# Causal self-attention inside a decoder layer: score units handled four at a time, eight slots of exponentials

## The reference

```python
q = (xq @ wq.T + bq).reshape(Bq, Tq, H, hd).transpose(0, 2, 1, 3)
...
scores = jnp.einsum('bhqd,bhkd->bhqk', q, k) / jnp.sqrt(jnp.asarray(hd, xq.dtype))
scores = scores + bias[None]            # relative position, and -inf above the diagonal
attn = jax.nn.softmax(scores, axis=-1)
out = jnp.einsum('bhqk,bhkd->bhqd', attn, v)
```

## Time and profile before

| | |
|---|---|
| median of 3 runs | 2869.88 us (2867.36 to 2872.76) |
| the profiled execution | 2871.87 us |
| its span in the trace | 2870.0 us |
| TensorE matmul busy | 2732.3 us (95% of the span) |
| VectorE busy | 1600.8 us (56%) |
| ScalarE busy | 1238.6 us (43%) |
| mean granted TensorE clock | 0.979 of full speed |

### The profile page before, as it was taken

How to read it: one execution, slowest core, us unless ns; L and a number is a source line. 1 busy time by engine, 2 the same in 40 slices (tenths; PEclk the granted TensorE clock), 3 DMA queues, 4 the chain that set the end, 5 groups by cost and what they waited for, 6 DMA issues and landing times. The chain is left out here.

```text
span 2870.0 us, 40053 instructions
## 1 busy us (share of the span) xinstructions
PE 2732.3 (95%) x12704; PEld 1797.9 (63%) x12704; DVE 1600.8 (56%) x3852; ACT 1238.6 (43%) x2624; POOL 410.2 (14%) x494
## 2 busy tenths in 40 slices
PE   7999969999999999999999889899989999999998
PEld 6788844444444444444444467667767778777877
DVE  5554356777777777777777188467632222122211
ACT  2322113555555555555555344498822222332222
POOL 4000021000000000000000422188555000000000
PEclk9999978999999999999999999899999999999999
DMA  7656563222222222222221587645331000000000
GB/s 223 225 181 195 184 150 78 66 67 67 68 68 68 68 69 68 68 68 67 67 67 25 120 229 223 213 150 170 125 121 44 15 30 30 30 0 30 30 15 15
DMA packets 137822, 272.53 MB, mean 95 GB/s; under 512 B 24773, under 2 KB 54725, under 8 KB 132362
## 3 DMA queue, kind: packets, MB, share of 16 engines
q1 hardware_dynamic: 132394, 254.57, 31.1%
q0 software_dynamic: 5216, 15.33, 1.9%
HBM read 175.44 MB, written 99.98 MB: 96 GB/s over the span
## 5 line engine op out<-in xcount | busy, mean ns | idle before, releaser
L1140 ACT ACTIVATE sa_pr<-sa_st 128x512 f32<-128x512 f32 (+3 forms) x1280 | 610.6, 532 | 562.2 <-DVE sa_st L1203 316.3
L1108 PE MATMUL sa_ov<-sa_pr,sa_v 128*33 128x512 f32 (+3 forms) x2560 | 537.7, 541 | 0.0
L1189 DVE TENSOR_REDUCE sa_part<-sa_mp 128x1 f32<-128x512 f32 (+3 forms) x768 | 411.8, 583 | 116.2 <-PE sa_mp L1089 115.0
L1099 PE MATMUL sa_st<-sa_q,sa_k 97*128 97x512 f32 (+3 forms) x1280 | 442.1, 414 | 16.6 <-ACT sa_pr L1140 13.1
L1099 PEld LDWEIGHTS sa_st<-sa_q,sa_k 97*128 97x128 f32 x1280 | 217.2, 190 | 318.8 <-ACT sa_pr L1140 211.3
L1089 PE MATMUL sa_mp<-sa_k,sa_q 96*128 96x512 f32 (+3 forms) x1280 | 373.5, 386 | 26.0 <-DVE sa_mp L1167 20.2
L1841 PE MATMUL ff_o<-ff_w,ca_q 128*128 128x512 f32 x1536 | 379.7, 396 | 3.4 <-DVE ca_q L1894 3.4
L1186 DVE CUSTOM_DVE_ANT_0 sa_mp<-sa_mp,sa_ub 128x512 f32<-128x512 f32 (+3 forms) x512 | 317.7, 663 | 79.3 <-PE sa_mp L1089 68.4
L1894 DVE TENSOR_TENSOR ca_q<-ca_v,ca_q 128x512 fp32r<-128x512 f32 x128 | 93.3, 729 | 474.6 <-ACT ca_q L1877 474.6
L130 PE MATMUL ff_f<-ff_ln_hi,ff_w 128*128 128x512 f32 x1024 | 340.9, 394 | 3.5 <-DVE ff_ln_lo L255 3.5
L1841 PEld LDWEIGHTS ff_o<-ff_w,ca_q 128*128 128x128 f32 x1536 | 287.1, 188 | 74.4 <-DVE ca_q L1894 3.6
(11 more groups left out here) (198 smaller groups left out, 3302.1 us busy)
## 6 DMA issues: line engine op xcount, KB each, us to landing
sa_q<-scratch_q SPq DMA_DIRECT2D x96, 256.0 KB, 8.3
sa_k<-scratch_k SPq DMA_DIRECT2D x96, 256.0 KB, 8.9
scratch_q<-qkv_qst SPq DMA_DIRECT2D x32, 512.0 KB, 7.2
scratch_k<-qkv_qst SPq DMA_DIRECT2D x32, 512.0 KB, 5.7
scratch_q<-sao_qst SPq DMA_DIRECT2D x32, 512.0 KB, 3.8
ca_q<-scratch_q SPq DMA_DIRECT2D x32, 512.0 KB, 4.2
scratch_v<-qkv_vst SPq DMA_DIRECT2D x8, 1056.0 KB, 5.2
sa_v<-scratch_v SPq DMA_DIRECT2D x16, 528.0 KB, 12.9
```

Source lines behind the costliest of these rows:

```text
L1099: pe.matmul(st[bank(u, h)][:, 0:w], ks[n.par][:, h, kb * P:(kb + 1) * P], qs[n.par][:, h, g * GW + c0:(g + 1) * GW], start=True, stop=True ...
L1108: last = pe.matmul(ov[64 * h:64 * h + VW, c0:GW], vs[n.par][:, kb, h, :], pr[:, u % 4, h, 0:GW - c0], start=(u in opens), stop=(u in ends))
L1140: act.activation(pr[:, u % 4, h, 0:w], st[bank(u, h)][:, 0:w], ACT.Exp, scale=SCALE).then_inc(s["exp"], 1)
L1189: dve.tensor_reduce(to, tile, AX_X, ALU.max).then_inc(s["red"], 1)
```

## The change

Units are handled in blocks of BATCH = 4 in place of 2, on all three engines: scores(u+4) with the max steps of u, scores(u+5) with those of u+1, and so on to scores(u+7), then the values of u to u+3. Eight slots of exponentials take the place of four, so exponent(u) waits for values(u-8). Three of the eight lie in `early[5]`, five in a tile of their own. Four units open the first slot in place of two. The number of score banks (3), the tables and the steps after each unit stay as they are.

```diff
+    BATCH = 4
...
-        for v in (u + 2, u + 3):
+        for v in range(u + BATCH, u + 2 * BATCH):
...
-        pr = k.sb(f"{name}_pr", [P, 4, 2, GW])
+        own = k.sb(f"{name}_pr", [P, 2 * BATCH - 3, 2, GW])
+        pr = [early[5][:, 2 * GW * i:2 * GW * (i + 1)].rearrange("p (h t) -> p h t", h=2) for i in range(3)]
+        pr += [own[:, i] for i in range(2 * BATCH - 3)]
...
-                                     pr[:, u % 4, h, 0:GW - c0], start=(u in opens), stop=(u in ends))
+                                     pr[u % len(pr)][:, h, 0:GW - c0], start=(u in opens), stop=(u in ends))
...
-            scores(Step(0, 0, UNROLL), 0)
-            scores(Step(0, 0, UNROLL), 1)
+            for u in range(BATCH):
+                scores(Step(0, 0, UNROLL), u)
 
             def slot(n, left):
-                for u in range(0, NU, 2):
+                for u in range(0, NU, BATCH):
                     ahead = list(after(n, u, left))
-                    for i in range(2):
+                    for i in range(BATCH):
                         if ahead:
                             scores(*ahead[i])
                         for m, a in steps_at(n, u + i, left):
                             max_step(m, a)
-                    values(n, u)
-                    values(n, u + 1)
+                    for i in range(BATCH):
+                        values(n, u + i)
...
-                waits(act, s["av"], NU * n + u - 2)
+                waits(act, s["av"], NU * n + u - (2 * BATCH - 2))
...
-                    act.activation(pr[:, u % 4, h, 0:w], st[bank(u, h)][:, 0:w], ACT.Exp, scale=SCALE).then_inc(s["exp"], 1)
+                    act.activation(pr[u % len(pr)][:, h, 0:w], st[bank(u, h)][:, 0:w], ACT.Exp, scale=SCALE).then_inc(s["exp"], 1)
...
             def slot(n, left):
-                for u in range(0, NU, 2):
+                for u in range(0, NU, BATCH):
                     for m, v in after(n, u, left):
                         exponent(m, v)
-                    if u + 1 in ends:
-                        empty(n, u + 1)
+                    if u + BATCH - 1 in ends:
+                        empty(n, u + BATCH - 1)
...
-            bias(Step(0, 0, UNROLL), 0)
-            bias(Step(0, 0, UNROLL), 1)
+            for u in range(BATCH):
+                bias(Step(0, 0, UNROLL), u)
 
             def slot(n, left):
-                for u in range(0, NU, 2):
+                for u in range(0, NU, BATCH):
                     ahead = list(after(n, u, left))
-                    for i in range(2):
+                    for i in range(BATCH):
                         if ahead:
                             bias(*ahead[i])
                         for m, a in steps_at(n, u + i, left):
                             reduce(m, a)
```

More of the change, by code:

```diff
@@ L1146, in empty @@
                 act.activation(osb[:, g % 2, :], ov[:], ACT.Copy).then_inc(s["out"], 1)
-            exponent(Step(0, 0, UNROLL), 0)
-            exponent(Step(0, 0, UNROLL), 1)
+            for u in range(BATCH):
+                exponent(Step(0, 0, UNROLL), u)
             def slot(n, left):
-                for u in range(0, NU, 2):
+                for u in range(0, NU, BATCH):
                     for m, v in after(n, u, left):
                         exponent(m, v)
-                    if u + 1 in ends:
-                        empty(n, u + 1)
+                    if u + BATCH - 1 in ends:
+                        empty(n, u + BATCH - 1)
             run(act, N, slot, UNROLL)
```

## The result

The changed kernel takes 3129.89 us (3128.54 to 3134.07, 4 runs); the kernel before took 2871.32 (2867.36 to 2874.51, 4 runs). The ratio is 1.0904, 95% interval 1.0885 to 1.0923: 9.0% slower. The forecast was 3,005, range 2,945 to 3,060. The sign was right and the size was not. The profiled execution has a span of 3129.2 us. Lines numbered above 914 moved down by one to three: exponentials are L1143, scores L1102, max matmuls L1092, values L1111, reductions L1192 and L1189, bias L1206.

The account below looks back on a forecast made before the run. TensorE was taken to bound the kernel at full clock. Added bank waits less saved switches, 14 x 9.0 us, plus 4 and 5 for the last and first slots, gave +135 us: 3,005, range 2,945 to 3,060.

Parts of the forecast that it names:

- What bounds the kernel: In mid self-attention TensorE sets the pace, busy 493.8 of 500 us at full clock, with VectorE at 78%.
- what the change removes: Ten of a slot's 20 round trips between scores and values go, saving 3.5 us per slot, 56 us in 16.
- switch price: One round trip on TensorE from scores to values and back costs 0.35 us beyond the matmuls' usual pitch.
- Waits for a bank: In blocks of four, later score tiles wait for three score banks; a slot becomes 81.9 us, 9.0 more.
- third chain (c): Max steps wait for VectorE's reductions two steps back, 0.61 us per head; four in a row without values run into it.
- third rival: TensorE's idle moments lower its clock to 0.87, adding 8.7 us in each of 14 slots: 3,127 us; chance 0.05.
- last slot: Self-attention's final slot: TensorE waits in every block yet keeps clock 1.00, cited against a falling clock; +4 us forecast.
- t6: A block's sixth score tile; in block 28 it needs the third tile's bank and starts at 3.11 us, not 1.9.
- The other parts: Copy-outs and exponential slots outside the block waits cost nothing; the last slot adds 4 us, the first 5.

Follow-up runs that it names:

- fours_turn: The changed kernel with one max step moved from u = 9 to u = 5, so block 8 holds one step fewer: 3126.8 us.
- fours_fill_turn: The changed kernel with repeated, overwritten max matmuls as filler inside blocks and one max step moved from u = 9 to u = 5: 3037.1 us.
- fours_4banks: The changed kernel with four score banks in place of three and three single max banks in place of two double ones: 3162.1 us.
- pairs_4banks: Blocks of two with eight slots of exponentials, four score banks and three single max banks: 2950.4 us, ratio 1.0280 to the kernel before.
- fours_fill: The changed kernel with the next max step's matmul repeated four times in a block's wait, 492 more matmuls in all: 3053.8 us.
- pairs_8slots: The kernel before, blocks of two, but eight slots of exponentials, three of them in early[5]: ratio 0.9997 to the kernel before.

## Why the prediction was wrong, point by point

**What bounds the kernel, what the change removes.** Right in kind. The switch price of 0.35 us was read from the gaps; with almost nothing left to wait for, ten fewer switches gave 1.7 us per slot, not 3.5. Twice too much, at most. It did not fail the forecast, which adds up whole blocks.

**Waits for a bank.** Right to 0.16 us in eight of ten blocks; the last two are off by 0.25 and 0.23 us in opposite directions, so that the sum comes out the same is partly luck. From the first score to the first value, at full clock (block 20 is read from fours_turn, where it isn't touched):

```
u                0     4     8     12    16    20    24    28    32    36    sum
forecast         5.55  4.7   5.85  4.75  3.95  6.05  4.75  5.2   4.9   5.7   51.4
measured         5.54  4.68  5.91  4.85  3.79  6.00  4.89  5.16  5.15  5.47  51.4
```

With 30.4 us of values and their switches (30.5 in the trace of fours_fill_turn) this makes 81.9 us. Of the 17.85 us that a slot got longer, 8.4 are these waits less the switches saved (forecast 9.0, against 72.9 for the slot before; the mean before was 73.48).

**Which bank.** The prediction named the score banks; fours_4banks and pairs_4banks show that with one max bank fewer the max side costs more than the fourth score bank gives. The third chain (c) of the prediction was in the sum, but the text read it as the lesser one.

**The clock.** This is the step that failed. The sum took a clock of 1.00, and so put the clock's loss at nothing, and the third rival, "the clock falls as well", had 0.05. Its price was 3,127 us, from 8.7 us per slot at a mean clock of 0.87. Measured: 3129.9, with 91.33 - 81.9 = 9.4 us per slot at 0.89. The whole adds up: 14 x 8.4 us of waits, 14 x 9.4 of clock and 8 us in the outer slots are 257 of the 258. The price was right in kind, and its closeness partly luck (9.4 for 8.7 made up for 8.4 in place of 9.0); the chance was wrong. fours_fill and fours_fill_turn show the cause: more matmuls in the idle moments, and the clock and 76 to 93 us come back (the 93 include the moved step, for which fours_turn alone shows 3 us).

Why was the chance so low? It rested on the last slot, where TensorE waits in every block at a clock of 1.00. But no wait of a matmul there is over 0.5 us, and all of its blocks but one (2.5 us, from 1576.27) have values after 1.7 us at the latest. The same trace held a nearer case, which I had not read. At the edge of the loop, TensorE stands still for 1.75 us (timeline and busy time by stretch, kernel before):

```profile
1040.88 0.45 PE L1099 MATMUL sa_st<-sa_q,sa_k 97*128 97x128 f32 x2 [1.75 <-issue]
...
1043.11 2.78 PE L1108 MATMUL sa_ov<-sa_pr,sa_v 128*33 128x512 f32 x8
```
```profile
1038.00:1043.10 5.10, 3.09 (x14) 1.32 (x10) 2.76 (x9) 1.65 (x5) 0.00 (x0) 1.00 0.15 40
1043.10:1046.50 3.40, 3.40 (x11) 1.15 (x11) 1.70 (x4) 0.87 (x2) 0.00 (x0) 0.50 0.26 67
```

Then 3.4 us at the lower level follow, and eight value matmuls take 2.78 us where they take 1.91 in the earlier trace rows. The prediction itself foresaw a wait of 1.2 us in block 28 (t6 at 3.11 in place of 1.9) in each slot. With this row, one in twenty was far too little for the clock's fall. It would not have made it certain either: pairs_8slots stands still for 1.42 and 0.66 us at the same edge, and its clock stays at 1.00 (timeline and busy time by stretch):

```profile
1034.01 0.45 PE L1103 MATMUL sa_st<-sa_q,sa_k 97*128 97x128 f32 x2 [1.42 <-issue]
...
1035.81 0.44 PE L1103 MATMUL sa_st<-sa_q,sa_k 97*128 97x384 f32 x1 [0.66 <-ACT ca_pq L1144]
```
```profile
1030.00:1036.00 6.00, 3.81 (x17) 1.49 (x16) 4.00 (x14) 2.45 (x7) 0.00 (x0) 1.00 0.12 34
1036.00:1042.00 6.00, 6.00 (x31) 3.05 (x31) 4.98 (x14) 3.26 (x7) 0.00 (x0) 1.00 0.55 145
```

The Trainium skill ("TensorE: Matmul & The Clock Gate", A second HAM failure mode) describes a kernel in which TensorE idles briefly between groups of matmuls that cycle through PSUM banks, so that its clock goes up and down and throughput is lost. This trace agrees: a mean of 0.89 in 600 to 1500 us, with several falls and returns in every slot. The prediction cited the section and let one counterexample outweigh it.

**The other parts.** Slots of exponentials and copy-outs cost nothing, as said (pairs_8slots). First and last slot together cost 8 us (258 less 250); 9 were forecast.

**The range.** It was built from the waits' uncertainty alone, which was small and well judged. The clock's case lay outside it as a whole.

## What to carry to other kernels

Grouping like work saves switches, but it takes away the pauses in which the other engines catch up; before you group, work out how far the producer can run ahead (here seven banks, most of them emptied only through VectorE's queue) and compare it with the work between two pauses. When a change adds waits to a TensorE that was hardly ever idle, cost them twice: as waits, and as matmuls at the lower clock after them; look in the trace of before for its longest stand-still and what the clock did next. And where waits come from an engine that is late altogether, don't count on another queue order or on a bank taken from elsewhere: the one order and the one split tried here both made it worse, and less work for that engine helped at once.

## What the runs showed of the hardware

More matmuls made the kernel faster: 492 useless ones took 76 us off, since the clock stayed up. And whether the clock fell depended on more than the block's own waits: blocks with the same work and the same 5.9 to 6.0 us (733.7 and 1007.6 us above) went into the values once at the lower clock and once at the full one. With one step moved, block 8 was 1.2 us shorter and its values still ran at the lower clock in most slots, and the time at the lower level stayed the same (21.5 against 21.0 us per slot). Even a stand-still at the loop's edge was followed by a fall in one kernel (1.75 us, before) and by none in another (1.42 and 0.66 us, pairs_8slots). So here the clock's loss can't be taken from one block's shape; it is read for a whole stretch.
